# A mixture-of-experts stage in two parts of eight batches, with 64 virtual experts

## What is computed

```python
h = _layernorm(x, axis=-1) * (1 + ca) + sa
x = x + ga * _L0_attn_ref(h, ...)            # attention with bias, softmax, and an MLP
h = _layernorm(x, axis=-1) * (1 + cb) + sb
x = x + gb * _L0_ffn_ref(h, ...)             # the experts
# _L0_ffn_ref, T = 4096 tokens, E = 32 experts, K = 4:
scores = sigmoid(x @ gate_w.T)
_, topk_ids = top_k(scores + e_bias, K)
topk_w = scores[topk_ids] / sum over the 4
a = silu(x @ w1[e]) * (x @ w3[e]) * topk_w   # 96 wide, for the 4 experts of a token
out = sum over the 4 of a @ w2[e]
```

## Time and profile before

| | us |
|---|---|
| median of 3 runs (654.62 to 656.91) | 655.31 |
| the profiled execution | 654.79 |
| its span, first to last instruction | 652.9 |

### The profile page before, as it was taken

How to read it: one execution, slowest core, us unless ns; L and a number is a source line. 1 busy time by engine, 2 the same in 40 slices (tenths; PEclk the granted TensorE clock), 3 DMA queues, 4 the chain that set the end, 5 groups by cost and what they waited for, 6 DMA issues and landing times.

```text
span 652.9 us, 15761 instructions
## 1 busy us (share of the span) xinstructions
PE 466.8 (71%) x4460; PEld 364.0 (56%) x4461; DVE 429.4 (66%) x1404; ACT 325.0 (50%) x732; POOL 388.7 (60%) x620
## 2 busy tenths in 40 slices
PE   3457999989899877778878731207999999980067
PEld 0234666666666655666666621006998989970046
DVE  5776888888888873758897886101666666661037
ACT  1236887888888884365554531004666656420000
POOL 5565666666666410446777777760677777777700
PEclk9977999999999999999987855557999999995579
DMA  7998000000006006111111112515555544511188
GB/s 203 272 292 208 2 1 0 0 0 0 0 2 259 3 2 194 38 38 47 60 60 59 59 57 73 181 64 121 134 134 136 146 127 138 148 54 52 52 332 315
DMA packets 68852, 66.29 MB, mean 102 GB/s; under 512 B 8912, under 2 KB 60336, under 8 KB 68800
## 3 DMA queue, kind: packets, MB, share of 16 engines
q1 hardware_dynamic: 52096, 43.64, 23.2%
q0 software_dynamic: 8192, 17.84, 7.7%
q10 hardware_dynamic: 8512, 4.20, 2.3%
HBM read 40.86 MB, written 27.93 MB: 105 GB/s over the span
## 4 chain that ended last, share of the span: by engine, by line
PE 30%; DVE 23%; issue 20%; POOL 13%; DVEq 6%; DMA 4%; ACT 3%; POOLq 1%; SPq 1%; ACTq 0%
POOL xs L659 9%; DVE L L1379 7%; PE PS L991 5%; PE PS L1111 4%; PE PS L1014 3%; DVE yidx L1759 3%; PE PS L1099 3%; PE PS L966 3%; POOL ys L677 3%; PE PS L1300 2%; DVEq L335 2%; PE PS L994 2%; DVE YQ L1757 2%; ACT hid L795 2%; PE PS L1030 2%
## 5 line engine op out<-in xcount | busy, mean ns | idle before, releaser
L659 POOL DMA_INDIRECT xs<-YQ,posi x128 | 123.6, 965 | 76.7 <-issue 64.2
L677 POOL DMA_INDIRECT ys<-YQ,yidx x128 | 122.7, 959 | 59.6 <-issue 34.8
L1379 DVE TENSOR_TENSOR L<-PS,BIAS 128x768 f32<-128x768 f32 x128 | 116.6, 951 | 24.5 <-PE PS L994 22.0
L725 ACT ACTIVATE PR<-L 128x768 f32<-128x768 f32 x128 | 105.9, 842 | 45.3 <-DVE L L1379 39.7
L1757 DVE SCALAR_TENSOR_TENSOR YQ<-PS,tag,YQ 128x128 f32 x160 | 56.1, 350 | 46.5 <-DVE yidx L1759 30.4
L1231 PE MATMUL PS<-BIAS,V 128*128 x320 | 63.2, 342 | 4.0 <-issue 2.0
L991 PE MATMUL PS<-YQ 32*128 32x256 f32 x512 | 46.7, 434 | 17.5 <-DVE L L1379 16.2
L1231 PEld LDWEIGHTS PS<-BIAS,V 128*128 128x128 f32 x320 | 52.1, 193 | 11.1 <-issue 11.1
L1223 PE MATMUL PS<-ident,PR 128*128 128x128 f32 x160 | 25.0, 281 | 31.9 <-DMA PR<-xs 31.9
L873 ACT ACTIVATE L<-PS 128x384 f32<-128x384 f32 x40 | 19.6, 491 | 54.2 <-PE PS L1231 54.2
L886 ACT ACTIVATE V<-PS 128x512 f32<-128x512 f32 x40 | 23.9, 597 | 44.4 <-PE PS L1223 44.4
(11 more groups left out here) (275 smaller groups left out, 1112.4 us busy)
## 6 DMA issues: line engine op xcount, KB each, us to landing
PR<-xs SPq DMA_DIRECT2D x160, 72.0 KB
BIAS<-ys SPq DMA_DIRECT2D x12, 512.0 KB, 8.2
modb<-mod_rows SPq DMA_DIRECT2D x1, 4096.0 KB, 14.1
dist_rep<-dist_row SPq DMA_DIRECT2D x4, 768.0 KB, 8.3
xs<-pad_row SPq DMA_DIRECT2D x33, 72.0 KB, 13.1
xs<-pad_row SPq DMA_DIRECT2D x1, 2304.0 KB, 18.2
X<-in_x ACTq DMA_DIRECT2D x4, 512.0 KB, 6.4
BIAS<-dist_rep SPq DMA_DIRECT2D x4, 512.0 KB, 9.0
```

Source lines behind the costliest of these rows:

```text
L659: pool.indirect_dma_start(out=xs, out_offset=bass.IndirectOffsetOnAxis(ap=posi[j][:, t * TOPK + k:t * TOPK + k + 1], axis=0), in_=ROWS[j][ ...
L677: pool.indirect_dma_start(out=ys, out_offset=bass.IndirectOffsetOnAxis(ap=yidx[:, n:n + 1], axis=0), in_=YQ[:, n * D:(n + 1) * D], in_offs ...
L725: act.activation(PR[u % 4][:, :], L[u % 2][:, :], ACT.Exp).then_inc(s["exp_done"], 1)
L1379: return dve.tensor_tensor(L[u % 2][:, :].rearrange("p (j w) -> p j w", j=2), PS[:, at:at + 2, 0:HW], BIAS[:, u, :].rearrange("p (j w) -> ...
```

## The change

The expert stage is made of two parts of eight batches. Each part has its own 32 regions in `xs`, so there are 64 *virtual experts*, and a second-part row's expert number is raised by 32. PE counts each part in columns of its own in bank 6. The first eight batches hold 8 * 256 * 4 = 8192 rows, exactly 64 slots. There are now 128 + 64 = 192 passes in 48 steps. The tables are 64 wide, and one new step turns a virtual expert's number back into a real one. The zero rows behind the first part's counts are written by SP during the routing, as soon as batch 8 is placed. SP loads the first sixteen steps without waiting for the second part's scatters. The 32 zero-row DMAs of the second part now stand in SP's list between those loads: 16 behind the first four steps' loads, then 8 and 8. In the last stage the first eight batches are read back when all passes are done and the first 64 slots are stored, and the wait for all slots comes at batch 8.

```diff
+PARTS = 2
+FIRST_PART = 8
+NV = PARTS * NE
+REGION = max(FIRST_PART, NB - FIRST_PART) * SEQ + P
+DUMMY = NV * REGION
+XTILES = NT * TOPK + NV
...
-            sp.dma_start(bass.AP(xs.tensor, NB * SEQ * DW, [[DW, P], [REGION * DW, NE], [1, DW]]),
-                         pad_row[:, :].unsqueeze(1).to_broadcast([P, NE, DW])).then_inc(s["zero_done"], 16)
+            sp.dma_start(bass.AP(xs.tensor, (REGION - P) * DW, [[DW, P], [REGION * DW, NV], [1, DW]]),
+                         pad_row[:, :].unsqueeze(1).to_broadcast([P, NV, DW])).then_inc(s["zero_done"], 16)
...
             sp.wait_ge(s["pad_ready"], 1)
-            for g in range(NE // 8):
-                for row in load_many(mybir.EngineType.SP, pads, g * 8, DUMMY):
+            def zero_behind(first):
+                for row in load_many(mybir.EngineType.SP, pads, first, DUMMY):
                     sp.dma_start(xs[bass.ds(row, P), :], pad_row[:, :]).then_inc(s["pad_done"], 16)
+            for first in range(0, NE, 8):
+                zero_behind(first)
             sp.wait_ge(s["t_ready"], 1)
...
             first, second = rows_at(0), rows_at(2)
             for i in range(GROUP):
-                sp.wait_ge(s[f"scat{i}"], 16 * NT * TOPK // GROUP)
+                sp.wait_ge(s[f"scat{i}"], 16 * TPB * TOPK * FIRST_PART // GROUP)
             sp.wait_ge(s["pad_done"], 16 * NE)
             load_pair(first, 0)
             load_pair(second, 2)
-            with sp.Fori(0, XSTEPS // 4 - 1) as four:
-                i = four * 4
+            def load_four(i):
                 for pair in range(2):
                     rows = rows_at(i + 2 * pair + 4)
                     sp.wait_ge(s["xt_ev"], i + 2 * pair + 2 + 2)
                     load_pair(rows, 2 * pair)
-            for g in range(SLOTS // 16):
-                sp.wait_ge(s[f"yst{g}"], 16 * 16 * LIVES)
+            sp.wait_ge(s["pad_ready"], 2)
+            early = FIRST_PART * TPB * TOPK // (4 * XG) - 1
+            for i in range(early):
+                for first in range(NE, NV, 8):
+                    if (first - NE) // 8 == i or i == 0 and (first - NE) // 8 >= early:
+                        zero_behind(first)
+                load_four(4 * i)
+            for i in range(GROUP):
+                sp.wait_ge(s[f"scat{i}"], 16 * NT * TOPK // GROUP)
+            sp.wait_ge(s["pad_done"], 16 * NV)
+            with sp.Fori(early, XSTEPS // 4 - 1) as four:
+                load_four(four * 4)
             sp.wait_ge(s["y_ev"], XG * (XSTEPS + 2))
             for b in range(NB):
                 r = b % len(G)
+                if b in (0, FIRST_PART):
+                    slots = (FIRST_PART if b == 0 else NB) * TPB * TOPK
+                    for g in range(SLOTS // 16):
+                        sp.wait_ge(s[f"yst{g}"], 16 * 16 * (slots // SLOTS + (1 if g < slots % SLOTS // 16 else 0)))
...
# PE
             def ranks(b, n):
+                half = part_of(b)
                 pe.wait_ge(s["r_mask"], b + 1)
-                if not at(b, 0):
-                    all_before(n + 1)
-                    count(1, rest, OH[(n + 1) % 2][:, 1, :, :])
+                if b > 0:
+                    all_before(n + 1, part_of(b - 1))
+                if b not in (0, FIRST_PART):
+                    count(2 * half + 1, rest, OH[(n + 1) % 2][:, 1, :, :])
...
             pe.wait_ge(s["tv_ready"], 1)
+            pe.wait_ge(s["h2_copies"], NB)
...
# DVE, pick: the cast of the indices becomes an add of half * NE
# DVE, place:
+                if b == FIRST_PART:
+                    dve.scalar_tensor_tensor(pads[:, 0:NE], iota_v[0:1, 0:NE], float(REGION), PS[0:1, 6, 0:NE],
+                                             ALU.mult, ALU.add).then_inc(s["pad_ready"], 1)
# DVE, table: cnt, pads, ends, endi, edge, part, upto, lead, tend, ge, gl, gp, gt are 64 wide, and
+            st(dve.tensor_scalar(over[:, :], tv[:, 0:2], float(NE), float(-NE), ALU.is_ge, ALU.mult))
+            st.wait()
+            dve.tensor_tensor(tv[:, 0:2], tv[:, 0:2], over[:, :], ALU.add)
```

More of the change, by code:

```diff
@@ L202, in build @@
         group_no = sb("group_no", [P, 2])
[L204 to L217, removed]
+        cnt = sb("cnt", [P, NV])
+        pads = sb("pads", [1, NV], I32)
+        over = sb("over", [P, 2])
+        ends = sb("ends", [P, NV])
+        endi = sb("endi", [P, 2, NV], I32)
+        edge = sb("edge", [P, 2, NV])
+        part = sb("part", [P, NV])
+        upto = sb("upto", [P, NV])
+        lead = sb("lead", [P, NV])
+        tend = sb("tend", [P, NV])
+        onesf = sb("onesf", [P, NV])
+        ge = sb("ge", [P, 2, NV])
+        gl = sb("gl", [P, 2, NV])
+        gp = sb("gp", [P, 2, NV])
+        gt = sb("gt", [P, NV])
         late = sb("late", [P, 2])
@@ L270, in build, with part_of @@
         pairs = [pair_of(2 * k, 2 * (k % 2)) for k in range(NPAIR)]
+        def part_of(b):
+            return 0 if b < FIRST_PART else 1
         def all_turns(eng, turn, entered=False):
@@ L1144, in count, with all_before @@
                 return last
-            def all_before(n):
-                count(0, rest, OH[n % 2][:, 0, :, :])
-                return count(0, onesb, OH[n % 2][:, 1, :, :])
+            def all_before(n, half):
+                count(2 * half, rest, OH[n % 2][:, 0, :, :])
+                return count(2 * half, onesb, OH[n % 2][:, 1, :, :])
             def ranks(b, n):
+                half = part_of(b)
                 pe.wait_ge(s["r_mask"], b + 1)
-                if not at(b, 0):
-                    all_before(n + 1)
-                    count(1, rest, OH[(n + 1) % 2][:, 1, :, :])
-                count(0, tri, OH[n % 2][:, 0, :, :], start=at(b, 0))
-                count(1, onesb, OH[n % 2][:, 0, :, :])
-                count(1, tri, OH[n % 2][:, 1, :, :]).then_inc(s["r_rank"], 1)
+                if b > 0:
+                    all_before(n + 1, part_of(b - 1))
+                if b not in (0, FIRST_PART):
+                    count(2 * half + 1, rest, OH[(n + 1) % 2][:, 1, :, :])
+                count(2 * half, tri, OH[n % 2][:, 0, :, :], start=at(b, 0))
+                count(2 * half + 1, onesb, OH[n % 2][:, 0, :, :])
+                count(2 * half + 1, tri, OH[n % 2][:, 1, :, :]).then_inc(s["r_rank"], 1)
             def turn(products, rows, places, nxt, k, used):
@@ L1610, in pick @@
                 step.wait()
-                step(dve.tensor_copy(ids.rearrange("p (t k) -> p t k", t=TPB), topi[:, :, 0:TOPK]))
+                half = part_of(b)
+                step(dve.tensor_scalar(ids.rearrange("p (t k) -> p t k", t=TPB), topi[:, :, 0:TOPK], float(half * NE), None,
+                                       ALU.add))
                 step.wait()
                 dve.tensor_tensor(OH[j % 2][:, :, :, :].rearrange("p t k e -> p (t k) e"),
-                                  iota_e[:, :].unsqueeze(1).to_broadcast([P, TPB * TOPK, NE]),
+                                  iota_v[:, half * NE:(half + 1) * NE].unsqueeze(1).to_broadcast([P, TPB * TOPK, NE]),
                                   ids.unsqueeze(2).to_broadcast([P, TPB * TOPK, NE]), ALU.is_equal
@@ L1675, in _ @@
             dve.wait_ge(s["cnt_pe"], 1)
-            st(dve.tensor_copy(cnt[:, :], bank(6, NE)))
+            st(dve.tensor_copy(cnt[:, :].rearrange("p (h e) -> p h e", h=PARTS),
+                               bank(6, PARTS * TPB * NE).rearrange("p (h t e) -> p h t e", h=PARTS, t=TPB)[:, :, 0, :]))
             st.wait()
-            dve.scalar_tensor_tensor(pads[:, :], iota_e[0:1, :], float(REGION), cnt[0:1, :], ALU.mult, ALU.add
+            dve.scalar_tensor_tensor(pads[:, NE:], iota_v[0:1, NE:], float(REGION), cnt[0:1, NE:], ALU.mult, ALU.add
                                      ).then_inc(s["pad_ready"], 1)
@@ L1702, in _ @@
             st.wait()
-            st(dve.tensor_tensor(gl[:, :, :], ge[:, :, :], lead[:, :].unsqueeze(1).to_broadcast([P, 2, NE]), ALU.mult))
+            st(dve.tensor_tensor(gl[:, :, :], ge[:, :, :], lead[:, :].unsqueeze(1).to_broadcast([P, 2, NV]), ALU.mult))
             st(dve.tensor_reduce(tv[:, 0:2], ge[:, :, :], AX_X, ALU.add))
```

15 lines of the change are left out of this document (6 added, 9 removed).

## The result

The changed kernel takes 635.12 us (median, 633.34 to 638.09), the kernel before 655.4 us on the same chip: ratio 0.9693, 95% interval 0.9649 to 0.9736. The forecast was 635.0 with a range of 626 to 645. The profiled execution took 636.18 us, its span is 634.1. The lines of the changed kernel stand some 10 to 37 further down: zero rows are L434, loads L449, read-back L487, scatters L685, stores L703, row transposes L1252, the row numbers L1796.

What follows compares the result with a forecast made beforehand. Bound before: scatters, 21 us of expert-pipeline fill, store train, read-back. Forecast: step 47 at 436.3 + 0.8 + 2 + 146.8 + 0.5 = 586.4, last pass 601.0, read-back 31.1 from 601.3, span end 632.4, plus 1.9 and 0.5: 634.8, given as 635; range 626 to 645.

Steps and rivals of the forecast that it cites:

- the ring: Clear in step 26 waits for POOL's first 64 stored slots, 523 against 522.5: cost 0.5 us, bounds 0 and 5.
- The start: Table at 411.8, first load at 413.6, step 0's first transpose at 417.3, 26.1 us earlier than before.
- The moved zero rows: Sixteen zero rows issued ahead of step 4's load take 9.5 us and put step 4 at 436.3: cost 5.8 us.
- The clock: PE's pause of some 7 us ahead of step 4 may lower its clock: cost 2 us, bounds 0 and 3.
- The last stage: Read-back from 601.3 takes 31.1 us; last stores land near 608, hidden behind eight reads ending at 613, 5 to spare.
- The rule on the port: Skill's rule: DVE's port lock would make 17 scatters beside expert work take some 42 us more; the forecast didn't follow it.
- The hold-up costs nothing: Rival at step 4: SP's lead absorbs the zero rows and the clock stays up; 626 us, chance 0.07.
- POOL is the bound again: Rival in the store train: groups arrive late, gaps delay the second eight batches; 640 us, 644 with ring stalling, chance 0.12.
- Slower by blocked zero rows: Rival in SP's issuing: zero rows block, 1.22 us per issue eats the gain; 655 and more, say 660, chance 0.04.
- It doesn't start early: Rival at the expert stage's start: an overlooked wait holds the first load until 439.7; 661 us, chance 0.03.
- Scatters stretch: Rival in POOL's last 17 scatters: each takes 0.25 us longer beside DVE, store train 4 later; 639 us, chance 0.04.
- signs of being wrong: A gap elsewhere than step 4, an interval of steps other than 3.41, or a second wait at batch 8.

Runs made afterwards that it cites:

- Early start taken back: Changed kernel, but the first load of expert rows waits for all 128 scatters, not the first 64: 663.45 us, ratio 1.0092 to the kernel before.
- Zero rows moved: Changed kernel, but the second part's zero rows go out eight ahead of the first load, then 8, 8, 8, not 16, 8, 8: 630.91 us, ratio 0.9600.
- Ring of eight: Both edits on the changed kernel: stores counted in eight groups of 8 slots, not four of 16, and zero rows issued in eights: 632.06 us, ratio 0.9618.
- early read-back taken back: Changed kernel, but the first read-back waits for all 128 slots to be stored (the late read-back): 642.31 us, ratio 0.9776.
- repeated change: The changed kernel run again with nothing altered: 636.89 us, ratio 0.9686 to the kernel before.

## Why the prediction came out

By its own steps, forecast and measured in the profiled execution, in us:

| step | forecast | measured |
|---|---|---|
| table ready | 411.8 | 411.3 |
| first load | 413.6 | 412.7 |
| step 0 | 417.3 | 416.6 |
| step 3 | 427.1 | 427.2 |
| step 4, behind 16 zero rows | 436.3 | 435.7 |
| clock after that hole | +2 | +1.8 (step 4 to 5 took 5.15, not 3.36) |
| later zero rows | +0.8 | +1.4 (steps 8 and 12) |
| pace of the steps | 3.41 | 3.39: (588.54 - 435.70 - 1.8 - 1.4 - 4.0) / 43 |
| the ring | +0.5 | +4.0 |
| step 47 | 586.4 | 588.5 |
| last pass | 601.0 | 602.7 |
| first read to end | 31.1 | 31.4 |
| end of span | 632.4 | 634.1 |

**The start.** Right to 1 us. The register reads took 1.4 instead of 1.8, the wider table 0.5 instead of 1. The doubled fill of the regions' ends cost nothing, as taken: the first scatter begins at 264.6 (265.5 before). *Early start taken back* shows that each us here is one at the end.

**The moved zero rows.** Right: 5.2 late for 5.8. *Zero rows moved* shows the cause, and that they needn't cost this: what hurts is 16 issues in a row ahead of a load whose predecessors have no lead, and the fall of the clock that the hole brings.

**The clock.** 2 forecast, 1.8 measured. The pause was shorter than the 7 us of the forecast: PE stood idle for 5.0 us, up to 435.7. The granted clock fell to 0.5 (1.2 GHz) at 433.1, within the pause, and stayed there until 439.9.

**The ring: the term that was mis-sized.** 0.5 forecast, 4.0 measured. The forecast had the clear due at 522.5 and POOL through with 64 slots at 523. The clear was due at 525.88 - 3.62 = 522.3, but the stores were in only at 525.9. Two things made them late. The first store began at 441.5 and not at 440, after 3.85 of waiting for DVE's first four slots. From there POOL kept its 1.265 for sixty slots, and then the last group of four wasn't ready: it began at 519.51, after 2.50 of waiting for DVE, where the pace alone gives 517.3. The forecast had set 1.28 us per slot from the steps against 1.265, and as means both were right, but slots don't take passes evenly. Counting the rows that this routing gives each expert, the last experts with rows in the first part have 45, 43, 10 and 31, so slots 62 and 63 take 3 and 4 passes (one of these seven for an expert without rows), and the last group of four slots 9 instead of the mean 6. That is 2.2 of the 3.62 of waiting. The other 1.4 would have been there with even slots too. Step 30 is 3.2 late and the next one 0.8, at half clock: 4.0. The last group before a border of the ring should have been laid out pass by pass, not by a mean, and the start of the train from DVE's first slots. *Ring of eight* confirms the mechanism (the wait goes) and refutes the worth that I gave it on the way: removing 3.7 brought 2.0 of steps, and no time.

**The last stage.** Right in its length (31.4 for 31.1), and *early read-back taken back* shows the 5.9 of stores behind it, but the reserve was smaller than I had it. The last store was issued at 606.2 and was in at 612.0, 5.8 later, and not at 608. In the kernel with the late read-back, where no read runs beside it, the same store took 2.3 (606.33 to 608.63); in the traces of the moved zero rows, of both edits and of the repeated change it took 5.2 to 5.8 again. So stores land some 3 us later beside eight reads in flight. By the forecast's own 613 for the end of those reads, 1 us of the 5 was left. It was enough: the share of the DMA engines stays at 1.01 to 1.06 from 606 to 628.

**The rule on the port.** The forecast left the 17 scatters at 1.26 us beside DVE's expert work. In the change, from 420 to 440:

```profile
420.00:440.00 20.00, 14.04 (x75) 13.23 (x74) 4.52 (x18) 8.76 (x18) 13.42 (x15) 0.76 0.66 176
```

POOL made 15 instructions, as many as before with DVE idle, and began the last scatter at 436.7 (437.1). DVE is busy only 4.5 of these 20 us, so this stretch alone would be weak; with the zero rows moved, DVE was busy 2.62 of 4 us in 436 to 440 (the row shown there), as in full steps, and the last scatters and first stores began at 436.56, 437.82, 439.08 and 440.35, 1.26 apart. So this DVE work costs POOL nothing. It doesn't test what the Trainium skill (SBUF — State Buffer, "SBUF: two separate sides") says of GpSimd's descriptors, which is about DVE operations in a two-port mode. DVE ran SCALAR_TENSOR_TENSOR and TENSOR_TENSOR there and one COPY of 128x8 a step (0.16 us), and no row shows the mode of any of them.

**The rivals.** *The hold-up costs nothing* fell with the hole at step 4. *POOL is the bound again* half came: POOL did wait for its groups (13 us in all), but its last store began at 606.2, and the stores were in at 612.0, not at 618; only the ring felt it. *Slower by blocked zero rows* fell: 0.6 per issue beside scatters and loads. *It doesn't start early* fell, and cost 663 when it was brought about. *Scatters stretch* fell.

**The signs.** All five signs of being right came: the first transpose at 416.6, 5.2 at step 4 ended by a DMA, 3.85 between POOL's trains, SP's long wait on the last pass, 31.4 from the first read to the end. But two of the signs of being wrong came too, the gap at step 30 and the wait of 5.3 at batch 8: the sum was right with one term too small, and the second wait was already in its own numbers, since eight reads are issued in some 4 us and the stores were to land at 608.

So step 47 came 2.1 later than the sum: +3.5 (ring), +0.6 (later zero rows), -0.6 (step 4), -0.2 (clock) and -1.2 (43 steps at 3.39). The profiled execution was 1.9 above its forecast of 634.3. That the median was hit to 0.1 is luck: the profiled execution lay 1.1 above the median, where the kernel before's lay 0.5 below, and the repeated change, at 636.9, would have missed by 1.9.

## What to carry to other kernels

Where an engine's train of transfers is the only bound, work added to other engines is free up to the lead that they have, and not a step further: measure that lead first (31 us here, of which 8 steps took 28), since it is what an earlier start lets you spend. Instructions moved into an issuing queue cost most where the loads behind them have no lead yet; eight ahead of the first load and eight at a time behind it cost 4.2 to 6.0 us less in all than sixteen at once. And where a mean rate of one engine just matches another's, look at the uneven piece at the border where somebody waits, not at the mean. A store that is to hide behind reads lands later because of them (5.8 us here, 2.3 without), so its reserve has to be worked out with that.

## What the chip showed unasked

- The same program can take 24% longer on some chips (811 and 806 us against 655): in the traces of its variants there, engines resume late at single places, mostly by 3 to 13 us, from some 20 us after POOL's first scatter on. Only PE's busy time is longer, at a lower mean clock (537.2 against 496.9 us).
- A wait removed from the path of a well-fed engine may not give back its length: PE has gaps of 0.5 to 0.8 us where its loop turns, and a wait before them hides them.
- A pause of PE cost 0.8 to 1.8 us more after it had ended, since the next step ran at half clock: 5.15 for 3.36 after 5.0 us of standing, 4.12 after 2.35 and 4.76 after 2.80 (in the repeated change).
